# A transformer on one core: the rows of queries and keys of a visit loaded in two pieces instead of four, with new places for all work

## The reference

```python
NL, D, H, DFF = (6, 128, 16, 512)          # HD = 8
for i in range(NL):
    xn = _adaln(x, noise_emb, n1_w[i], n1_b[i])
    q, k, v = jnp.split(xn @ qkv_w[i].T, 3, axis=-1)
    q, k = _rope(q.reshape(B, L, H, HD)), _rope(k.reshape(B, L, H, HD))
    x = x + _attn(q, k, v, src_mask).reshape(B, L, D) @ so_w[i].T
    xn = _adaln(x, noise_emb, n2_w[i], n2_b[i])
    q = _rope((xn @ cq_w[i].T).reshape(B, L, H, HD))
    k = _rope((context @ ck_w[i].T).reshape(B, LC, H, HD))
    x = x + _attn(q, k, v_of_context, ctx_mask).reshape(B, L, D) @ co_w[i].T
    xn = _adaln(x, noise_emb, n3_w[i], n3_b[i])
    x = x + (jax.nn.gelu(xn @ f1_w[i].T + f1_b[i], approximate=False) @ f2_w[i].T + f2_b[i])
```

## Time and profile before

| | us |
|---|---|
| median of 3 runs | 2144.84 (2144.1 to 2145.57) |
| the profiled execution | 2146.84 |
| its span | 2145.0 |

### The profile page before, as it was taken

The page is one execution under the profiler, slowest core; times in us unless marked ns, Lnnn a source line. Parts: engine busy times, 40 slices in busy tenths (PEclk is TensorE's granted clock), DMA queues, the critical chain, the costliest instruction groups (busy, mean ns, idle before and its releaser), DMA issues.

```text
span 2145.0 us, 40593 instructions
## 1 busy us (share of the span) xinstructions
PE 1786.5 (83%) x13134; PEld 767.5 (36%) x13138; DVE 1719.4 (80%) x4125; ACT 1514.2 (71%) x2810; POOL 1035.6 (48%) x1506
## 2 busy tenths in 40 slices
PE   3654277168899999999999999999999999999652
PEld 2332266012333333333343334333343333333222
DVE  7677111579899998999999998999989999998677
ACT  2442021037788998888998888988888998888553
POOL 2554531734445564545654555554545555534432
PEclk9676589569999999999999999999999999999775
DMA  3001122232413334334333235233344333431100
GB/s 107 5 0 40 37 88 88 58 99 61 113 38 95 86 82 98 75 82 98 97 86 92 67 82 125 78 78 93 68 107 99 81 76 85 96 95 43 31 2 20
DMA packets 139788, 158.35 MB, mean 74 GB/s; under 512 B 39855, under 2 KB 107431, under 8 KB 137255
## 3 DMA queue, kind: packets, MB, share of 16 engines
q1 hardware_dynamic: 137535, 151.54, 28.5%
q0 software_dynamic: 2048, 4.20, 0.7%
HBM read 84.90 MB, written 68.38 MB: 71 GB/s over the span
## 4 chain that ended last, share of the span: by engine, by line
PE 68%; DVE 10%; POOL 5%; issue 3%; ACT 2%; DMA 1%; SPq 0%; POOLq 0%; DVEq 0%; ACTq 0%
PE ps L1379 16%; PE ps L1332 9%; PE ps L1343 9%; PE ps L1390 4%; PE ps L1481 4%; DVE smax L1900 4%; PE ps L1491 4%; PE ps L1455 3%; PE ps L1431 2%; PE ps L1415 2%; PE ps L1354 2%; PE ps L604 2%; PE ps L1448 2%; PE ps L614 2%; PE ps L1366 1%
## 5 line engine op out<-in xcount | busy, mean ns | idle before, releaser
L1608 ACT ACTIVATE big<-ps 128x512 f32<-128x512 f32 x1920 | 1006.7, 612 | 147.1 <-PE ps L1343 140.0
L1900 DVE TENSOR_REDUCE smax<-ps 128x1 f32<-128x512 f32 x1536 | 962.0, 682 | 88.9 <-PE ps L1332 82.0
L1379 PE MATMUL ps<-big,vaug 128*32 128x512 f32 x3072 | 411.2, 608 | 0.0
L1332 PE MATMUL ps<-k,q 49*128 49x512 bf16 x1536 | 291.2, 389 | 22.4 <-DVE smax L1900 16.7
L1343 PE MATMUL ps<-q,k 52*128 52x512 bf16 x1536 | 291.9, 385 | 8.5 <-DVE smax L1900 2.5
L1811 POOL CAST mparts<-smax 128x16 bf16<-128x16 f32 x96 | 19.2, 200 | 351.8 <-DVE smax L1900 351.8
L1908 DVE TENSOR_REDUCE maxima<-ps 128x4 f32<-128x308 f32 x384 | 155.7, 469 | 19.2 <-PE ps L1366 14.9
L1332 PEld LDWEIGHTS ps<-k,q 49*128 49x128 bf16 x1536 | 75.2, 94 | 251.6 <-DVE smax L1900 130.6
L1343 PEld LDWEIGHTS ps<-q,k 52*128 52x128 bf16 x1536 | 76.4, 94 | 204.3 <-issue 55.6
L1797 POOL TENSOR_TENSOR rot<-rot,cs 128x512 f32<-128x512 f32 x72 | 92.3, 1281 | 97.4 <-DVE rot L1919 97.3
L1802 POOL TENSOR_TENSOR hat<-rot,rparts 128x512 f32<-128x512 f32 x72 | 83.4, 1160 | 58.8 <-ACT rparts L1656 58.6
(11 more groups left out here) (312 smaller groups left out, 2938.9 us busy)
## 6 DMA issues: line engine op xcount, KB each, us to landing
k<-scratch_keys SPq DMA_DIRECT2D x192, 112.0 KB
q<-scratch_queries SPq DMA_DIRECT2D x192, 96.0 KB
cq<-scratch_cross_queries SPq DMA_DIRECT2D x48, 384.0 KB, 5.8
scratch_keys<-rparts SPq DMA_DIRECT2D x48, 192.0 KB, 2.9
scratch_queries<-rparts SPq DMA_DIRECT2D x48, 192.0 KB
scratch_cross_queries<-rparts SPq DMA_DIRECT2D x48, 192.0 KB
scratch_keys<-rparts SPq DMA_DIRECT2D x48, 128.0 KB, 2.4
scratch_queries<-rparts SPq DMA_DIRECT2D x48, 128.0 KB
```

The source lines that it names most:

```text
L1332: last = nc.tensor.matmul(out[u], m.q6[rows, v % 2, 2 * g + pr, qt * P:(qt + 1) * P], m.k6[rows, v % 2, 2 * g + pr, :], start=True, stop=True)
L1379: last = nc.tensor.matmul(m.ps[32 * j:32 * j + 32, pv_bank, :], of_head(m.vaug, v % 2 * TB + kt, g, j), of_quad("self", q)[:, j, :], start ...
L1608: nc.scalar.activation(of_quad(kind, p // 2)[:, p % 2 * 2 + u, :], bank("exp" if kind == "self" else "cross exp", p, u), ACT.Exp, scale=sc ...
L1900: nc.vector.tensor_reduce(m.smax[:, n % 2, qt, u, pr:pr + 1], bank("max", i, u), AX.X, ALU.max).then_inc(s_read["self"], 1)
```

## The change

`PIECES` goes from 4 to 2. Each load of rows is then twice as long: four pairs, 2048 columns, 4 KB a row, so the four DMAs of a piece move 832 KB (852 kB) instead of 416 KB. A visit has two pieces and eight of these DMAs. PE waits for them at steps 0 and 16 of a visit's 32 instead of 0, 8, 16 and 24; the waits of a piece on the one two before it are gone with the third and fourth pieces. A piece waits for half of the scores of visit v - 2 instead of a quarter.

With it all places have new numbers: `STARTS`, `OFFSETS`, `LAYER_OFFSETS`, `BLOCK_PLACES` and the places of the first stages that lie beside the layers. The instructions on each engine are the same in kind and number, apart from SP's loads; the order differs. The diff, cut to its core:

```diff
-PIECES = 4
+PIECES = 2
 PIECE = PAIRS // PIECES
...
 OFFSETS = {
...
-    "SP load cross": (114836,),
-    "SP load rows": (-37813, -33135, -27137, -10113),
...
+    "SP load cross": (115341,),
+    "SP load rows": (-33130, -15037),
```

More of the change, by code:

```diff
@@ L868 @@
[L868 to L880, removed]
@@ L890 @@
[L890 to L904, removed]
@@ L905 @@
[L905 to L918, removed]
@@ new lines @@
+    "PE turn maxima": (-10825, -690, 22684, 35300),
+    "PE cross turn maxima": (130097,),
+    "PE gather": (49411, 67887),
+    "PE cross gather": (145046, 149046),
+    "PE turn on": (72386,),
+    "PE cross turn on": (151858,),
+    "PE project": (76213,),
+    "PE cross project": (154304,),
+    "PE turn cross": (96077,),
+    "PE turn ff": (163862,),
+    "PE turn next": (-63333,),
+    "PE product cross": (99244,),
+    "PE product query": (-57228,),
+    "PE product key": (-59739,),
+    "PE values": (-26759,),
@@ new lines @@
+    "ACT copy maxima": (-9953, -164, 23549, 35943),
+    "ACT cross copy maxima": (130989,),
+    "ACT copy on": (73323,),
+    "ACT cross copy on": (152437,),
+    "ACT scale cross": (96336,),
+    "ACT scale ff": (164368,),
+    "ACT scale next": (-62133,),
+    "ACT first cross": (103739,),
+    "ACT second cross": (106640,),
+    "ACT first query": (-50858,),
+    "ACT second query": (-46976,),
+    "ACT first key": (-53978,),
+    "ACT second key": (-49061,),
+    "ACT copy values": (-26016,),
@@ new lines @@
+    "POOL rotate cross": (101428,),
+    "POOL less cross": (106230,),
+    "POOL third cross": (106887,),
+    "POOL rotate query": (-50888,),
+    "POOL less query": (-48270,),
+    "POOL third query": (-44182,),
+    "POOL rotate key": (-56599,),
+    "POOL less key": (-50710,),
+    "POOL third key": (-47687,),
+    "SP rows": (-2355, 12660, 30793, 40240),
+    "SP cross rows": (133805,),
+    "SP store cross 0": (105650,),
+    "SP store cross 1": (107699,),
+    "SP store cross 2": (111458,),
@@ L940 @@
-    "PE gain next": -65318,
-    "DVE gain next": -63388,
-    "PE context values": 118173,
-    "ACT copy context values": 121205,
-    "SP load context": 98185,
-    "PE product context": 63338,
-    "DVE rope context": 64483,
-    "POOL rotate context": 69436,
-    "ACT first context": 71901,
-    "POOL less context": 73618,
-    "ACT second context": 75124,
-    "POOL third context": 78636,
-    "SP store context": 93713,
+    "SP weights self": 59700,
+    "SP weights context": -34493,
+    "SP weights out": 149653,
@@ new lines @@
+    "SP weights ff": 120154,
+    "SP weights next": -67877,
+    "PE gain cross": 75977,
+    "DVE gain cross": 76930,
+    "PE gain ff": 125243,
+    "DVE gain ff": 126118,
+    "PE gain next": -63625,
+    "DVE gain next": -63046,
+    "PE context values": 119239,
+    "ACT copy context values": 120855,
+    "SP load context": 99260,
+    "PE product context": 63258,
+    "DVE rope context": 63267,
+    "POOL rotate context": 68686,
+    "ACT first context": 71974,
+    "POOL less context": 83745,
@@ L953 @@
+    "ACT second context": 84489,
+    "POOL third context": 90679,
+    "SP store context": 97703,
 }
 BLOCK_PLACES = {
-    "SP block rows": (1464321, 1496859),
-    "SP block weights": (1430696,),
-    "DVE block weight sums": (1471184,),
-    "PE block weights": (1485433,),
-    "DVE block weight scale": (1488201,),
-    "DVE block ternary": (1493466,),
-    "DVE block begin": (1446859, 1507626, 1618100, 1715462),
-    "POOL block root first": (1449311, 1507947, 1618754, 1720965),
-    "DVE block first": (1460660, 1513632, 1620684, 1723603),
@@ L988 @@
-    "DVE block output": (1953321, 2209427, 2320561, 2535691),
-    "SP block store": (2352727, 2485755, 2744925, 2753501),
+    "SP block rows": (1457724, 1532401),
+    "SP block weights": (1456528,),
+    "DVE block weight sums": (1469124,),
+    "PE block weights": (1485862,),
+    "DVE block weight scale": (1487047,),
+    "DVE block ternary": (1495515,),
+    "DVE block begin": (1445728, 1506416, 1585810, 1714521),
+    "POOL block root first": (1456242, 1511073, 1613789, 1731638),
+    "DVE block first": (1459043, 1513043, 1617073, 1738997),
```

162 lines of the change are left out of this document (77 added, 85 removed), and 12 rows, old and new, of the table OFFSETS.

## The result

The changed kernel takes 2176.7 us (2173.1 to 2179.0, 4 runs), the kernel before 2144.5 us in the same comparison. The ratio is 1.0149, with a 95% interval of 1.0132 to 1.0167: slower by 32 us. The forecast was 2183 us.

What follows compares the result with a forecast made beforehand. PE was taken as the bound, busy 1189.85 of 1203.00 us in the steady stretch. Terms +38.9 + 1.0 - 1.5 - 0.6 = +37.8 us on the median of 2144.84 gave 2183 us, range 2145 to 2202.

Steps and rivals of the forecast that it cites:

- Nothing gained by fewer issues and waits: SP's issues per visit fall from 16 to 8 and PE drops two waits of four; counted as worth nothing.
- The delay D of `cq` behind the second piece: On SP's queue the piece is served before `cq`, delaying it 2.6 us; over 20 visits +38.9 us.
- the full-queue rows: Trace rates with the queue full: `cq` rows average 197 GB/s (D 2.6 us), 2-KB rows 166 to 174.
- the fast row: 2-KB rows of a piece issued alone: 234 GB/s, scaled to 334 in full flow; D 0.85 us, +8 us.
- `cq` is issued at the same moment: On SP the piece's four DMAs replace two row moves, 1.65 us for 1.60, so `cq`'s issue time stays.
- ScalarE and PE swap neighbours only: New places in the steady stretch: order nearly unchanged, counted as nothing, with bounds of -8 and +4 us.
- The first piece, +1.0 us: Next visit's first scores wait for the larger piece 0: five visits, 0.1 to 0.5 us each, +1.0 us.
- PE's waits on VectorE, -1.5 us: At L1332, PE's stalls let other engines get ahead, so half of 2.9 us of waits goes: -1.5 us.
- Fill and end: No term for filling the layers; at the end, shorter VectorE waits against swaps: -0.6 us, between -2 and +3.

Runs made afterwards that it cites:

- after_four_pieces: Changed kernel with four pieces again in their old order round the load of `cq`, all other new places kept: 2144.6 us, ratio 0.9997.
- after_cross_first: Changed kernel with the load of `cq` put ahead of the second piece again on SP, two pieces and other places kept: 2147.4 us, ratio 1.0011.
- before_second_ahead: Kernel before with two pieces, the second issued between stores and `cq` load, row moves ahead of the stores: 2212.1 us, ratio 1.0321.
- before_second_ahead_early_cast: before_second_ahead with ScalarE's first cast of the cross queries moved ahead of a pair of exponentials: 2177.0 us, ratio 1.0144.
- after_short_rows: Changed kernel with each piece's loads cut in two, eight loads with 2-KB rows instead of four with 4-KB rows: 2173.5 us, ratio 1.0132.
- after_late_cast: Changed kernel with ScalarE's first cast of the cross queries behind two pairs of exponentials instead of one: 2228.5 us, ratio 1.0382.
- before_fourth_ahead: Kernel before, four pieces, the fourth issued between stores and `cq` load, two row moves ahead of the stores: 2151.8 us, ratio 1.0032.

## Why the prediction was right

The sign, the place and the mechanism were right, and the total was off by 6 us (2183 against 2176.7). That it came so near is in part luck, since two misses stood against each other. By its own steps:

*Nothing gained by fewer issues and waits.* Right: after_four_pieces and after_cross_first differ by 2.8 us in favour of four pieces, which have more of both.

*The delay D of `cq` behind the second piece, 2.6 us.* Right: 2.8 us in before_second_ahead, where the places are the old ones, and a queue served at 202 GB/s. The choice between the bounds, the full-queue rows and not the fast row, was the decisive one. With 334 GB/s the term would have been +8 instead of +38.9 us, and the forecast some 2151 us. The 334 were scaled up from one window of 1 us; the first pieces before the change, at 184 GB/s in the mean, would have pointed the same way as the full-queue rows.

*"`cq` is issued at the same moment", and "ScalarE and PE swap neighbours only".* Wrong, and the largest miss. One of these neighbours was the cast at the head of the chain that leads to `cq`, and its swap gave 1.5 us in 17 of the 20 visits, worth 35 us by before_second_ahead and before_second_ahead_early_cast. I had followed the order of SP and PE into this place and not that of the engines that feed the stores. In the changed kernel the issue of `cq` in turn comes 0.8 us later behind the product than in after_cross_first, since the piece's four issues fill the gap, so of the head start half was left at the issue.

*PE's clock.* Not in the sum: 6.2 us in the changed kernel, 19 to 26 us in the slower runs. The row for it wasn't there, since no wait of the steady stretch before was long enough.

*The first piece, +1.0 us.* Mis-sized: 3.5 us of waits in four visits, and 2.8 us by the two runs that differ in it. (The "416 kB" of that step are 426 kB; its sum doesn't hang on it.)

*PE's waits on VectorE, -1.5 us.* Wrong in sign: they went from 2.9 to 5.5 us, in after_cross_first and after_four_pieces too, and stayed at 2.9 us in before_second_ahead with its 44 us of stalls. So this belongs to the new places, and stalls of PE take nothing off it.

*Fill and end.* The seven profiles with the new places reach the stretch at 627.8 to 632.3 us, the six with the old at 625.7 to 628.3. So the filling is on average 3 us longer with the new places, and the end is 2 to 3 us shorter (forecast 0 and -0.6).

So the sum came out near the result because one overlooked gain of some 35 us stood against a loss that, without it, is larger than I had made it: 67 us instead of 38, of which the waits at L1366 are 44 (forecast 38.9) and the clock 19 (forecast nothing). For before_second_ahead, where the gain is missing, I had expected 2175 us and the same sum gives 2183; it took 2212.

## What to carry to other kernels

Where one in-order queue feeds a transfer that the bound engine waits for, the bytes issued ahead of it count at the rate of the full queue, less their head start. Take that rate from whole loads or from several windows in a row: single windows of 1 us scattered from 147 to 258 GB/s here. When places are refitted, follow every engine of the chain that leads to that transfer back to the bound engine, since a swap of neighbours at its head moves all of it. And a stall of two microseconds on TensorE can cost more than its length, since the matmuls behind it may run at half the clock.

## What the runs showed of the hardware

The granted clock fell from 1.00 to 0.50 (1.2 GHz) behind many of the long waits of PE at the first cross score, and stayed there for some 3.4 us, in eight visits of the two slowest kernels and after_short_rows for 6.8 us, while PE worked on: in five of 20 visits of the changed kernel (waits of 1.8 to 2.6 us), in 12 of before_second_ahead, in 16 of after_late_cast. The length of the wait alone doesn't decide: in the changed kernel a wait of 1.95 us was followed by a clock of 1.00, in before_second_ahead one of 2.78 us, and in before_fourth_ahead one of 1.56 us by 0.60. Every wait of less than 1.5 us there kept 1.00, in the 20 visits of each of the thirteen kernels whose traces are compared. What else decides is not shown. It adds 6.2 us of matmul time to 24.5 us of idle time in the changed kernel, 18.9 to 43.7 and 25.9 to 57.8 in the two slowest.

Four loads of 192 to 224 KB, two into each half of the partitions, are done sooner when the halves take turns: their packets begin within 4.2 instead of 4.9 us when almost nothing else is in the queue, and the changed order of the same loads took 19 us off the kernel's time. Rows of 2 KB and of 4 KB into one half at a time moved at 184 and 176 GB/s.
